# Cross-attention with group norm on one core: every engine's steps written out in a straight line instead of a loop

## What is computed

```
q = conv1x1(Wq, bq, y); k = conv1x1(Wk, bk, y); v = conv1x1(Wv, bv, x)   # split into 8 heads of 16
attn = softmax(q k^T / sqrt(128), axis=-1)                               # (B, 8, 16, 16)
o = conv1x1(Wo, bo, attn v) + x
mu, var = mean and variance of o over all 128 x 1024 of a batch
out = (o - mu) * rsqrt(var + 1e-5) * gn_w + gn_b
```

## Time and profile before

| | before |
|---|---|
| median of 3 runs | 175.67 us |
| the profiled execution, its own time | 175.87 us |
| its span (first to last instruction) | 174.1 us |
| TensorE busy | 163.0 us (94%) |
| VectorE busy | 151.8 us (87%) |
| ScalarE busy | 135.8 us (78%) |
| GpSimd busy | 112.4 us (65%) |
| mean DMA rate | 291 GB/s |

### The profile page before, as it was taken

The page is one execution under the profiler, slowest core; times in us unless marked ns, Lnnn a source line. Parts: engine busy times, 40 slices in busy tenths (PEclk is TensorE's granted clock), DMA queues, the critical chain, the costliest instruction groups (busy, mean ns, idle before and its releaser), DMA issues. The chain is left out here.

```text
span 174.1 us, 4168 instructions
## 1 busy us (share of the span) xinstructions
PE 163.0 (94%) x997; PEld 129.2 (74%) x997; DVE 151.8 (87%) x555; ACT 135.8 (78%) x356; POOL 112.4 (65%) x166
## 2 busy tenths in 40 slices
PE   7989999999999999999999999999999999999730
PEld 7877888877777888877777778888777777785410
DVE  1786999999998999999999999999999999976551
ACT  4656588998878888798888888888988888776442
POOL 3287677877866777776787677767778777741020
PEclk9999999999999999999999999999999999999995
DMA  6998778999899999989999999999999866622223
GB/s 206 409 416 339 254 224 322 328 334 334 279 355 336 311 330 321 332 308 342 334 314 325 356 324 326 313 333 330 330 339 327 297 237 241 242 121 120 121 115 126
DMA packets 14265, 50.70 MB, mean 291 GB/s; under 512 B 1712, under 2 KB 1712, under 8 KB 14256
## 3 DMA queue, kind: packets, MB, share of 16 engines
q1 hardware_dynamic: 13968, 50.34, 81.0%
q10 hardware_dynamic: 288, 0.27, 0.5%
HBM read 33.82 MB, written 16.78 MB: 291 GB/s over the span
## 5 line engine op out<-in xcount | busy, mean ns | idle before, releaser
L514 PE MATMUL o_ps<-x_sb,m_sb 128*128 128x512 f32 x128 | 63.1, 615 | 0.0
L431 DVE TENSOR_TENSOR hl_sb<-y_sb,hl_sb 128x512 fp32r<-128x512 f32 x64 | 47.9, 749 | 1.7 <-ACT hl_sb L326 1.0
L271 POOL TENSOR_TENSOR rstd<-veps,nhalf 128x1 f32<-128x1 f32 x32 | 28.2, 882 | 24.5 <-DVE veps L436 24.5
L326 ACT CAST hl_sb<-y_sb 128x512 fp32r<-128x512 f32 x64 | 39.5, 620 | 1.8 <-DMA y_sb<-in_ctx_dram 1.8
L514 PE MATMUL g_ps<-hl_sb 128*128 128x258 f32 x256 | 38.6, 293 | 0.0
L366 ACT ACTIVATE out_sb<-o_ps,shift,gain 128x1024 f32<-128x1024 f32 (+1 forms) x32 | 38.3, 1197 | 0.1
L300 POOL TENSOR_TENSOR lsuma<-hl_sb 128x256 f32<-128x256 f32 x31 | 23.2, 749 | 22.9 <-DVE hl_sb L431 22.9
L514 PEld LDWEIGHTS o_ps<-x_sb,m_sb 128*128 128x128 f32 x128 | 22.1, 191 | 14.9 <-issue 14.0
L514 PEld LDWEIGHTS g_ps<-hl_sb 128*128 128x128 f32 x256 | 32.8, 190 | 0.0
L321 ACT ACTIVATE a_sb<-sc_sb,smin 128x128 f32<-128x128 f32 x32 | 12.9, 402 | 16.8 <-DVE smin L422 16.7
L287 POOL TENSOR_TENSOR lsum<-lsuma,lsumb 128x256 f32<-128x256 f32 x31 | 22.8, 737 | 4.1
(11 more groups left out here) (64 smaller groups left out, 297.6 us busy)
## 6 DMA issues: line engine op xcount, KB each, us to landing
y_sb<-in_ctx_dram SPq DMA_DIRECT2D x32, 512.0 KB, 5.1
x_sb<-in_x_dram SPq DMA_DIRECT2D x32, 512.0 KB, 5.6
out_dram<-out_sb SPq DMA_DIRECT2D x31, 512.0 KB, 4.8
out_dram<-out_sb SPq DMA_DIRECT2D x2, 256.0 KB, 2.2
w_in<-in_weights_dram ACTq DMA_DIRECT2D x1, 256.0 KB, 5.4
cols<-in_columns_dram ACTq DMA_DIRECT2D x1, 3.0 KB, 3.3
```

The costliest lines, as they stand in the source:

```text
L271: nc.gpsimd.tensor_tensor(rstd[:, h1:h1 + 1], veps[:, h1:h1 + 1], nhalf[:, :], ALU.pow).then_inc(rstd_ready, 1)
L326: nc.scalar.copy(hl_sb[:, k, chunks, 0:C], y_sb[:, k, chunks, :]).then_inc(h_ready, 1)
L431: nc.vector.tensor_tensor(hl_sb[:, ky, chunks, C:2 * C], y_sb[:, ky, chunks, :], hl_sb[:, ky, chunks, 0:C].bitcast(F32), ALU.subtract).the ...
L514: return nc.tensor.matmul(dst, lhsT, rhs, start=start, stop=stop, **more)
```

## The change

`pipeline` no longer opens a loop: all 37 steps of every engine are written out in order, with t0 and t as constants. The parameters `first` and `end` go away. The operations, their order on each engine, the waits and the values they wait for are the same.

```diff
-        def pipeline(eng, step, begin=0, first=2 * UNROLL, end=B):
-            for t in range(begin, first):
-                step(t - t % UNROLL, t % UNROLL)
-            with eng.Fori(first, end - UNROLL + 1, UNROLL) as t0:
-                for k in range(UNROLL):
-                    step(t0, k)
-            for t in range(end, B + LAGS):
+        def pipeline(step, begin=0):
+            for t in range(begin, B + LAGS):
                 step(t - t % UNROLL, t % UNROLL)
...
-            pipeline(sp, step, end=B - UNROLL)
+            pipeline(step)
...
-            pipeline(pool, step)
+            pipeline(step)
...
-            pipeline(act, step, first=3 * UNROLL)
+            pipeline(step)
...
-            pipeline(dve, step, begin=2)
+            pipeline(step, begin=2)
...
-            pipeline(pe, step)
+            pipeline(step)
```

## The result

The changed kernel takes 174.05 us (median of 8 runs, 173.57 to 175.35); the kernel before took 175.66 us in its 8 runs beside them (175.45 to 176.61). The ratio is 0.9895, 95% interval 0.9871 to 0.9919: faster by about 1%. The profiled execution took 174.09 us, with a span of 172.3 instead of 174.1.

The account below looks back on a forecast made before the run. TensorE was taken to set the pace at 4.73 us a step, VectorE 0.13 us behind. A gain of 2.03 - 0.15 - 0.30 = 1.58 us took the median from 175.67 to 174.1 us, range 173.5 to 175.7.

Parts of the forecast that it names:

- the case that came: Whole kernel: the forecast with its good end, 173.5 to 174.8 us, given a chance of 0.69.
- What bounds it: Steps without a jump: TensorE sets the pace, busy for all 4.73 us, with VectorE 0.13 us behind.
- The account of the steps: Steps 7 to 32: 120.28 us for 25 steps, 2.03 us above 4.73 each, split over entry, jumps and exit.
- the plain pace: Any step without a jump, in the loop or straight code: 4.73 us.
- The entry's 0.19: Loop entry, steps 8 to 10: three steps take 14.38 us, 0.19 us over.
- Each jump, 0.285: Four later jumps, steps 14 to 31: 1.14 us over, 0.285 each, put on TensorE's compare-and-branch and what it leaves behind.
- VectorE's stall in step 11, 0.15: Before the first jump: 0.15 us of the 0.62 over, taken as code run for the first time, not the loop's.
- Exit, 0.09: Loop exit, from step 31 to step 32: 4.82 us, 0.09 us over.
- New code, 0.30 for two stalls: Written-out steps 12 to 36: code executed once brings two more VectorE stalls, 0.30 us given back, from nothing to 0.6.
- TensorE's blocks: TensorE's 16 KB instruction packets: seven or eight instead of three, taken to cost zero, at most 1.26 us each.
- the rival that had TensorE wait for its blocks: Written-out code: six new instruction blocks each stall TensorE by 1.26 us, giving 181.4 us; chance 0.12.

Follow-up runs that it names:

- e10: The changed kernel measured again, nothing altered: 173.66 us median, ratio 0.9874 to the kernel before.
- e9: Changed kernel with extra tail matmuls on TensorE and VectorE's p_sb operation moved between bn_aggr and mrow: 174.21 us.
- e11: Changed kernel with GpSimd's last add of a step cut from 128 columns to one, plus a memset at the head of VectorE's code: 174.00 us.
- e4: Kernel before with only TensorE written out, the other engines keeping their loops: 174.70 us, ratio 0.993.
- e5: e1 with TensorE's wait for the next step's x block moved behind the current step's products with x: 174.46 us, ratio 0.9927.
- e3: Kernel before with only TensorE keeping its loop of four steps, the other engines written out: 174.86 us, ratio 0.9933.
- e1: Kernel before with rounds of 12 steps on TensorE, VectorE and GpSimd, 8 on ScalarE and SP, one jump each: 175.54 us, ratio 0.997.
- e6: Kernel before with ten one-column memsets added at the head of VectorE's code: 175.50 us, ratio 0.9981.
- e8: Changed kernel with ten small unread matmuls added on TensorE in steps 34, 35 and 36: 173.74 us, ratio 0.9882.

## Why the prediction was right, and where its steps were not

The time (174.1 against 174.05) and the sign held, and the case that came was the likeliest of those named. That the median was met to 0.05 us is luck: the same kernel again gave 173.66 (e10). The terms behind it fared unequally.

**What bounds it: right as far as it is shown.** TensorE is busy for the whole of a step (4.73 of 4.73 below), straight code with constants runs at the same 4.73 as code in a round, and VectorE's slack carries it. e9 and e11 moved VectorE's and GpSimd's work without moving the pace, so neither sets it. The account of the steps, 2.03 us above the plain pace, is right as well. The stretch came down by 1.88 of these: 0.08 are left at step 32, and 0.07 are the 4.733 of the other steps against 4.73. The entry's 0.19 was TensorE's loop: 0.03 is left in e4, which writes out TensorE alone, and 0.09 in e5.

**Each jump, 0.285: right size, wrong cause.** The prediction put it on TensorE's compare-and-branch of 210 ns and what it leaves behind. e3 keeps that branch and shows it hidden at step 16: its row starts there at 72.04, and TensorE's weight loads go on beside it at 72.13 and 72.24. What costs is about 0.15 of register instructions between TensorE's variance product and the products with x (e1 has it without the jump; e5 moves them, and 0.01 is left at step 16), and about 0.14 of VectorE's half, which belongs to a place in its code. The Trainium skill, "Advanced Engine Details and Errata", Control Flow Timing, has about 108 ns for a compare-and-branch; TensorE's row reads 210. The lesson of e3 is that neither of them was the price.

**VectorE's stall in step 11, 0.15: wrong.** The prediction left it out of the gain as code run for the first time, which would stay. It was also too small: with VectorE's loop but TensorE written out, steps 12 and 13 are 0.33 over (e4). It is gone; the changed kernel's VectorE in step 11:

```profile
49.05 0.16 DVE L431 TENSOR_SCALAR veps<-st_ps 128x1 f32<-128x1 f32 x1
49.12 0.68 DVE L426 TENSOR_TENSOR hl_sb<-y_sb,hl_sb 128x512 fp32r<-128x512 f32 x1
```

It was right that something happens there for the first time, but it came back in every round at the same place, for 0.13 instead of 0.36 (e6), and it went with the loop.

**Exit, 0.09: not TensorE's exit but VectorE's stall.** In the kernel before, one of the late `hl_sb` is in step 31. In e1, e5 and e6, where none is, step 32 keeps the plain pace, with the loop and its exit in place. Written out, step 32 still has 0.08. The changed kernel's VectorE in step 31:

```profile
143.71 0.16 DVE L431 TENSOR_SCALAR veps<-st_ps 128x1 f32<-128x1 f32 x1
143.93 0.69 DVE L426 TENSOR_TENSOR hl_sb<-y_sb,hl_sb 128x512 fp32r<-128x512 f32 x1
```

`hl_sb` is 0.22 behind `veps` where it is 0.07 in step 11 above. It is VectorE's 576th instruction, in e3, e8, e9 and e10 as well. In e11, with one memset more ahead, the 576th is `veps`, and now that one is late, 0.23 behind the row before it where it is otherwise 0.07:

```profile
143.51 0.08 DVE L418 DVE_READ_ACCUMULATOR2_ANT smin<- 128x1 f32 x1
143.74 0.16 DVE L432 TENSOR_SCALAR veps<-st_ps 128x1 f32<-128x1 f32 x1 [0.15 <-PE st_ps L510]
```

There it costs 0.02 at step 32. So the straight code too has a stall that belongs to a place.

**New code, 0.30 for two stalls: over-sized.** There is this one stall, for 0.08. TensorE's blocks cost nothing, as taken: 8 packets of 16 KB came (seven or eight were forecast). The queue is TensorE's, with 8 packets in e4, which writes out TensorE alone, and 3 in e3, which leaves it its loop. They came under DMA engines that were 0.85 busy in the step below, and the steps are 4.73. The changed kernel's busy times in one step, answering to the earlier trace rows:

```profile
86.74:91.47 4.73, 4.73 (x32) 3.77 (x32) 4.56 (x18) 4.19 (x11) 3.55 (x6) 1.00 0.85 320
```

The DMA view of the changed kernel for 60 to 140 us has four of the blocks (packets, MB, share of 16 engines):

```profile
q8 instruction: 4, 0.07, 0.3%
```

The steps in that stretch hold them and are 4.73 long, so the rival that had TensorE wait for its blocks, 181.4 us, is refuted. (Its sum counted six new blocks. Eight instead of three are five, which would have made it 180.1.) The trace agrees with the Trainium skill, "Runtime: NRT & Kernel Launch", Instruction fetch mechanics, which has the crossing of a block mostly hidden.

**Not foreseen: the tail.** In the profiled execution the clock fell some 4 us earlier and took back 0.20. This belongs to the execution and not surely to the change, since e11 ends without it.

The errors nearly cancel. The gain of the stretch was 1.88, not 1.58: 0.15 more from step 11 and 0.22 less given back, less 0.07 for a plain pace of 4.733. The head gave 0.13 by the scatter from run to run (step 7 starts at 29.64 in e3 and at 30.33 in e1), and the tail took 0.20.

**Open.** Why VectorE stalls at these places of its code is not settled. The 192nd and the 576th instruction are 384 apart, three times 128, but the 320th and the 448th of the changed kernel show no stall, and nothing was run to find out what the spacing means. Nor was it settled why the first jump costs more than the later ones: 0.25 at step 12 in e3 against 0.14, and in e1 0.31 at its only jump against 0.15 at the boundaries without one. There is something in a first jump that register work does not explain. A version with TensorE's mean product earlier in its order, the one thing that the last two experiments point to, was not tried. No kernel of these beats the changed one by more than the runs can tell.

## What to carry to other kernels

A periodic pause in a hardware loop need not be the jump: list the weight loads or operations around it and look between which two the gap opens, then move the register work of a wait to where the engine has long work ahead of it. Here that gave 0.86 us (e5 against e1), where writing everything out gave 1.88. Do not put a stall down to first-time code until you have looked at the same instruction in every later round. And look at one instruction's number across kernels: the stall of VectorE kept its number while the operation at that number changed.

## What the runs showed of the hardware

- One place in VectorE's code, its 192nd instruction, stalls it by 0.36 to 0.39 us the first time and 0.13 us in every round after, though no instruction packet moved in the loop kernel from 60 to 140 us. Ten instructions put in ahead move the stall by ten instructions (e6). In straight code the 576th is late by 0.15, and one instruction put in ahead moves that stall by one (e11).
- TensorE's taken branch has a row of 208 to 234 ns. At the later jumps it added nothing: a boundary is 0.16 us over with it (e3) and 0.15 without it (e1). Register work with a row of 42 ns, between the variance product and the products with x, cost that 0.15 us; behind the products with x it cost 0.01 (e5).
- The same work at the same distance from the end ran at 0.97 of the clock in one kernel and at 0.74 in the other, and the last product took 0.38 or 0.58 us by it.
- VectorE's 512-column `hl_sb` took 0.76 us while GpSimd added 128 columns beside it, and 0.68 when GpSimd added one.
